# Latent down weights multiplied into the up weights on the chip, in a fused attention and feed-forward layer

## The chip, the cores and the metric

The kernel runs on one core of one Trainium2 chip. The metric is the device time of one execution in microseconds. Every number comes from timed runs of the kernel before, or from one further execution taken with the profiler.

## The reference

One transformer layer on x of 2 x 1024 tokens and 512 features, in float32: attention with 32 query heads and 8 key/value heads of 128 features, x added and normalised, then a feed-forward part of 1376 hidden features with 4-bit weights, added and normalised again. The part that matters here:

```python
q    = (x @ Wq.T)                 # 32 heads
k_r0 = x @ Wkr.T                  # 512 rope features of the keys, rotated by cos and sin
c_kv = x @ Wdk.T                  # 512 latents
k_c  = c_kv @ Wupk.T              # 512 other features of the keys
v    = c_kv @ Wupv.T              # 1024 features of the values
k    = k_c and rotated k_r0, put together
out  = softmax(causal(q @ k.T / sqrt(128))) @ v @ Wo.T
```

## The kernel before

Every product is made in three passes. A float32 matrix is split into a high part, rounded to the type that TensorE multiplies, and a low part, the rest; `three_pass` (line 262) issues high x high, high x low and low x high into one bank of PSUM. Over 512 features, four chunks of 128, that is a **group** of 12 matmuls of 128x512. Each split is a copy on ScalarE (the high part) and a subtraction on VectorE or GpSimd (the low part).

The program is written engine by engine, with semaphores between them; each engine and SyncE's queue of DMAs works through its own list strictly in order. It has three stages: projections ("a"), attention ("b") and feed-forward ("c").

**Stage a** goes over four blocks of 512 tokens (`NBLK`; `END` is the last). For block t TensorE issues 20 groups (`GROUPS_A`): four latent groups (`a_latents`, CG), four of the rope keys (RG, weights `a_wkr`), four of the other keys from the latents (NG, weights `a_wupk`; both in `a_keys`), and eight of the values (VG, weights `a_wupv`; `a_values`). Group g goes to bank `g % a_RING` of `a_bank`, five banks, and `a_group` first waits until the bank has been read (`a_bank_free`).

```python
            def a_group(t, g, pairs):

                pe.wait_ge(a_bank_free, a_count(t, g))
                three_pass(nc, a_bank[g % a_RING], pairs).then_inc(a_mm, 1)
```

The latents are split from PSUM into `a_cs` by `a_c_hi` on ScalarE and `a_c_lo` on VectorE. The rope keys are rotated on VectorE (`a_rope`, into two slots `a_kf`), rounded on ScalarE (`a_rope_hi`) and their low parts made on GpSimd (`a_rope_lo`). The other keys are split by `a_nope_hi` and `a_nope_lo`, the values by `a_v_hi` and `a_v_lo`. Keys and values go to DRAM by SyncE in pieces of 512 KB, and each block's split x too, 2 MB (`a_store_k`, `a_store_v`, `a_store_x`). SyncE's list for a block is: load the next x, store this x, then the eight stores of keys and eight of values. After block 0 it also copies x into `y_d`, DRAM to DRAM.

At the very start twelve matmuls of zeros run, then the latents of block 0 chunk by chunk as x and `Wdk` arrive (`a_first_latents`).

**The hand-over to attention.** After the last block's keys TensorE multiplies the first four query heads (`queries`), in turn with the first three value groups. The queries go to banks `bank[0]` and `bank[1]`, which are not in `a_bank`; they need the first x back from DRAM (`load_xs`) and the query weights split (`w_lo`). SyncE, when it has stored block 2's values, loads the first keys and values, the tables, two query weights (256 KB each) and x, and stores the last x. The other two query weights come after the rope keys' stores:

```python
            for n in range(8):
                a_store_k(END, n)
                if n in (1, 3):
                    load_wq(0, 2 + n // 2)
```

ScalarE's list there is `hi_wq(0, 0)`, `hi_wq(0, 1)`, `a_rope_hi(END)`, `hi_wq(0, 2)`, `hi_wq(0, 3)`, `a_nope_hi(END)`, and GpSimd's is two weight splits, four rope splits, two weight splits.

Stage b then runs 16 turns (two batches by eight key/value heads), each of scores, softmax, transposes and products with the values and `Wo`; stage c is the feed-forward part.

Of the kernel before, what the change touches and what calls it, by code (L numbers as in the profile page):

```python
# [21 lines left out]
F32 = mybir.dt.float32  # L22
# [310 lines left out]
def layer(nc, x, xT, wqT, wkrT, wdkT, wupkT, wupvT, woT, w13p, s13p, w2p, s2p, cosT, sinT, shifts,  # L333
# [5 lines left out]
    with ExitStack() as ctx:  # L339
# [6 lines left out]
        def sem(name):  # L346
# [4 lines left out]
        a_wdk = at(24 * K, "a_wdk", [P, 2, DC, 512], F32R)  # L351
# [11 lines left out]
        a_cs = at(180 * K, "a_cs", [P, 2, DC, TB], F32R)  # L363
        a_later = at(76 * K, "a_later", [P, 2, DC, 512], F32)
        a_zero = at(180 * K, "a_zero", [P, 512], F32)
# [28 lines left out]
                  tps[0][:].rearrange("p j q -> p (j q)")]  # L394
# [3 lines left out]
        a_first_in = [(sem(f"a_x0_in{k}"), sem(f"a_wdk_in{k}")) for k in range(DC)]  # L398
        a_first_hi, a_first_lo = sem("a_first_hi"), sem("a_first_lo")
        a_wkr_in = [sem(f"a_wkr_in{k}") for k in range(DC)]  # L400
        a_wkr_hi, a_wkr_lo = sem("a_wkr_hi"), [sem("a_wkr_lo0"), sem("a_wkr_lo1")]
        a_w_in = [sem(f"a_w_in{n}") for n in range(3)]
# [3 lines left out]
        a_w_hi, a_w_lo, a_wd_lo = sem("a_w_hi"), sem("a_w_lo"), sem("a_wd_lo")  # L406
# [28 lines left out]
        LATE = [(wupkT, a_later[:, 0], lambda p: a_wupk[:, p]),  # L435
                (wupvT[:, :, 0:512], a_later[:, 1], lambda p: a_wupv0[:, p]),
                (wupvT[:, :, 512:1024], a_raw[:, 0], lambda p: a_wupv1[p][:])]

        CG, RG, NG, VG, GROUPS_A = 0, 4, 8, 12, 20
        END = NBLK - 1  # L440

# [130 lines left out]
        def _(sp):  # L572
            def a_weights():
                for k in range(DC):
                    sp.dma_start(a_xraw[:, k], xT[0, :, k]).then_inc(a_first_in[k][0], 16)
                    sp.dma_start(a_raw[:, 0, k], wdkT[:, k]).then_inc(a_first_in[k][1], 16)
                for k in range(DC):
                    sp.dma_start(a_raw[:, 1, k], wkrT[:, k]).then_inc(a_wkr_in[k], 16)
                sp.dma_start(LATE[0][1], LATE[0][0]).then_inc(a_w_in[0], 16)
# [212 lines left out]
            sp.wait_ge(a_w_lo, 1)  # L792
            sp.wait_ge(a_wd_lo, 2)
# [10 lines left out]
            sp.wait_ge(a_mm, GROUPS_A * (END - 1) + RG + 4 + a_MM0)  # L804
# [41 lines left out]
        def _(pool):  # L846
# [14 lines left out]
            def a_weight_lo(n):  # L861
# [992 lines left out]
```

## Time and profile before

| | us |
|---|---|
| median of 3 timed runs | 2386.08 |
| lowest and highest | 2385.03, 2389.29 |
| the profiled execution | 2387.51 |
| its span, first to last instruction | 2385.7 |
| TensorE's matmuls busy in it | 2370.0 |
| VectorE, ScalarE, GpSimd busy | 1427.1, 1621.0, 578.6 |

The profile is of one execution. PE is TensorE's matmuls and PEld its weight loads, DVE VectorE, ACT ScalarE, POOL GpSimd, SP SyncE; SPq is the DMA queue that it issues to. A row of a timeline gives the start, the duration and the engine, then the line of the program, the operation, what it writes and reads, and how many there were; brackets at the end give the idle time before it and what ended it. An arrow points from what is read to what is written. "b_sps", "b_tps" and "b_ps" are banks of PSUM. Consecutive matmuls overlap, so the start of the next tells the pace, not the duration of one.

### The profile page before, as it was taken

How to read it: one execution, taken by the hardware profiler on the slowest of the kernel's cores; microseconds unless marked ns; L12 is line 12 of the kernel's file. 1: busy time of each engine (PE TensorE's matmuls, PEld its weight loads, DVE VectorE, ACT ScalarE, POOL GpSimd, SP SyncE). 2: the span in 40 equal slices, each digit the busy share in tenths (PEclk: the TensorE clock that was granted, in tenths of full speed). 3: DMA queues.
4: the chain of work that ended last, by engine and by line, in shares of the span. 5: the costliest groups of instructions: out<-in, count | busy, mean ns of one | idle time of the engine just before them, and what ended most of it. 6: DMA issues, size and time to landing. Idle time of an engine off the chain costs nothing.

```text
span 2385.7 us, 41133 instructions
## 1 busy us (share of the span) xinstructions
PE 2370.0 (99%) x12028; PEld 1993.1 (84%) x12028; DVE 1427.1 (60%) x3780; ACT 1621.0 (68%) x3221; POOL 578.6 (24%) x453
## 2 busy tenths in 40 slices
PE   9999999999999999999999999999999999999998
PEld 7888888888888888888888888888888888888886
DVE  5334766666767676766666676767676674242332
ACT  4224878888888888887878888888888885122211
POOL 3002323233332323232323333232323220000000
PEclk9999999999999999999999999999999999999999
DMA  7867444434353444444434445354434435311110
GB/s 273 300 216 289 131 143 138 136 132 155 131 176 110 170 138 141 132 141 149 136 129 139 148 135 174 106 171 138 148 127 145 137 129 209 120 71 36 53 35 18
DMA packets 133255, 340.24 MB, mean 143 GB/s; under 512 B 13328, under 2 KB 30736, under 8 KB 122640
## 3 DMA queue, kind: packets, MB, share of 16 engines
q1 hardware_dynamic: 133200, 339.53, 42.2%
q8 instruction: 31, 0.51, 0.1%
q14 instruction: 24, 0.20, 0.0%
HBM read 232.00 MB, written 111.67 MB: 144 GB/s over the span
## 4 chain that ended last, share of the span: by engine, by line
PE 96%; issue 1%; DVE 1%; ACT 1%; DMA 1%; SPq 0%; POOL 0%; DVEq 0%; POOLq 0%
PE b_ps L267 45%; PE b_sps L267 34%; PE b_tps L1549 10%; PE b_ps L1608 3%; PE b_tps L1608 2%; PE b_tps L267 1%; DMA b_xs<-xs_d 0%; DMA a_raw<-in_wkrT 0%; PE b_sps L1558 0%; ACT b_pt L1050 0%; ACT b_sc L1035 0%; ACT b_sc L1029 0%; DVE c_n_stats L286 0%; DVE b_sc L1252 0%; DVE a_xs L1176 0%
## 5 line engine op out<-in xcount | busy, mean ns | idle before, releaser
L1270 DVE TENSOR_TENSOR b_pt<-b_tps,b_pt 128x512 fp32r<-128x512 f32 (+3 forms) x768 | 426.8, 556 | 301.6 <-ACT b_pt L1050 297.5
L267 PE MATMUL b_sps<-b_kt,b_qs 128*128 128x512 f32 (+4 forms) x2304 | 497.1, 343 | 0.2
L1035 ACT ACTIVATE b_sc<-b_sc,b_rinv 128x896 f32<-128x896 f32 (+7 forms) x512 | 396.1, 774 | 105.4 <-DVE b_rinv L1260 99.5
L267 PEld LDWEIGHTS b_sps<-b_kt,b_qs 128*128 128x128 f32 x2304 | 403.1, 188 | 55.8 <-issue 1.4
L1050 ACT ACTIVATE b_pt<-b_tps 128x512 fp32r<-128x512 f32 (+3 forms) x768 | 366.9, 478 | 119.1 <-PE b_tps L1549 117.6
L267 PE MATMUL b_ps<-b_xs,b_wq 128*128 128x512 f32 x1536 | 441.0, 407 | 0.5 <-DMA b_xs<-xs_d 0.5
L267 PE MATMUL b_ps<-b_pt,b_vt 128*128 128x512 f32 x1584 | 436.0, 402 | 0.3 <-DVE b_ys L1281 0.3
L267 PE MATMUL b_ps<-b_wo,b_ot 128*128 128x512 f32 x1536 | 423.9, 405 | 0.1
L1029 ACT ACTIVATE b_sc<-b_sc,b_nmax 128x896 f32<-128x896 f32 (+7 forms) x512 | 395.5, 772 | 40.2 <-DVE b_nmax L1252 37.1
L1252 DVE CUSTOM_DVE_ANT_0 b_sc<-b_sps,b_mask 128x896 f32<-128x896 f32 (+7 forms) x512 | 386.7, 755 | 16.1 <-PE b_sps L267 16.0
L1549 PE MATMUL b_tps<-b_ident,b_sc 128*128 128x128 f32 x2304 | 374.3, 272 | 1.4 <-DVE b_pt L1270 1.4
L1549 PEld LDWEIGHTS b_tps<-b_ident,b_sc 128*128 128x128 f32 x2304 | 291.6, 140 | 75.9 <-issue 5.3
L267 PEld LDWEIGHTS b_ps<-b_pt,b_vt 128*128 128x128 f32 x1584 | 284.3, 188 | 49.1 <-DVE b_ys L1281 0.5
L267 PEld LDWEIGHTS b_ps<-b_xs,b_wq 128*128 128x128 f32 x1536 | 273.7, 189 | 45.9 <-DMA b_xs<-xs_d 1.6
L267 PEld LDWEIGHTS b_ps<-b_wo,b_ot 128*128 128x128 f32 x1536 | 270.8, 189 | 43.5 <-DVE b_ys L1281 0.3
L878 POOL TENSOR_TENSOR b_qs<-b_qf,b_qs 128x512 fp32r<-128x512 f32 x124 | 160.5, 1294 | 394.1 <-ACT b_qs L1009 394.1
L874 POOL TENSOR_TENSOR b_sw<-b_sw,b_sin 128x512 f32<-128x512 f32 x128 | 165.7, 1295 | 360.1 <-ACT b_sw L1002 358.7
L267 PE MATMUL b_sps<-c_xs,c_up 128*128 128x512 f32 (+3 forms) x1056 | 247.5, 390 | 0.0
L267 PEld LDWEIGHTS b_sps<-c_xs,c_up 128*128 128x128 f32 (+1 forms) x1056 | 195.2, 185 | 43.7
L1338 DVE TENSOR_TENSOR c_hb<-b_sps,c_hb 128x512 f32<-128x512 f32 (+1 forms) x44 | 30.4, 691 | 193.6 <-PE b_sps L267 187.0
L1234 DVE TENSOR_TENSOR b_qf<-b_ps,b_cos 128x512 f32<-128x512 f32 x128 | 88.5, 691 | 85.3 <-ACT b_sw L1002 43.3
L887 POOL TENSOR_TENSOR b_wo<-b_wraw,b_wo 128x512 fp32r<-128x512 f32 x64 | 82.8, 1294 | 228.6 <-ACT b_wo L1023 228.6
(133 smaller groups left out, 2271.9 us busy)
## 6 DMA issues: line engine op xcount, KB each, us to landing
b_xs<-xs_d SPq DMA_DIRECT2D x32, 2048.0 KB, 9.1
b_ys<-y_d SPq DMA_DIRECT2D x128, 256.0 KB, 2.7
y_d<-b_ys SPq DMA_DIRECT2D x128, 256.0 KB, 3.0
k_d<-a_ks SPq DMA_DIRECT2D x32, 512.0 KB, 3.9
v_d<-a_vs SPq DMA_DIRECT2D x32, 512.0 KB, 3.1
b_kt<-k_d SPq DMA_DIRECT2D x64, 256.0 KB, 4.5
b_vt<-v_d SPq DMA_DIRECT2D x16, 1024.0 KB, 4.9
b_wraw<-in_wqT SPq DMA_DIRECT2D x64, 256.0 KB, 2.7
```

What stands on the lines that cost most here:

```text
L267: ins = nc.tensor.matmul(out, *every[n], start=(n == 0), stop=(n == len(every) - 1))
L874: nc.gpsimd.tensor_tensor(sw[:], sw[:], sinq[:, blk * TB:blk * TB + TB], ALU.mult).then_inc(sin_done, 1)
L878: nc.gpsimd.tensor_tensor(qs[:, blk, h, LO], qf[:], qs[:, blk, h, HI], ALU.subtract).then_inc(q_lo, 1)
L887: nc.gpsimd.tensor_tensor(wo[:, h, LO], wraw[:, h % 2], wo[:, h, HI], ALU.subtract).then_inc(w_lo, 1)
L1029: nc.scalar.activation(sc[:, slot, 0:w], sc[:, slot, 0:w], ACT.Exp, bias=nmax[:, slot:slot + 1], scale=-1.0, accum_out=rsum[:, slot:slot + ...
L1035: nc.scalar.activation(sc[:, slot, 0:w], sc[:, slot, 0:w], ACT.Copy, scale=rinv[:, slot:slot + 1])\
L1050: nc.scalar.activation(pt[:, u % PT_UNITS, HI, 0:nj, h * P:(h + 1) * P], tps[n % 2][:, 0:nj], ACT.Copy)\
L1234: nc.vector.tensor_tensor(qf[:], banks[bk], cosq[:, blk * TB:blk * TB + TB], ALU.mult)\
L1252: nc.vector.tensor_tensor_reduce(out=like_banks(sc[:, slot, 0:w], i), in0=both_banks(sps[c % 2], i), in1=like_banks(mask[:, S - w:S], i), ...
L1270: nc.vector.tensor_tensor(pt[:, u, LO, 0:nj, h * P:(h + 1) * P], tps[n % 2][:, 0:nj], pt[:, u, HI, 0:nj, h * P:(h + 1) * P], ALU.subtract) ...
L1549: last = nc.tensor.transpose(tps[n % 2][:, j], sc[:, c % S_RING, (j0 + j) * P:(j0 + j + 1) * P], ident[:])
L1608: last = nc.tensor.matmul(c_y[t], c_hs[0:w, f % 2, a, t * P:(t + 1) * P], c_w2[f][b][0:w], start=(f == 0 and k == 0), stop=(f == FT - 1 an ...
```

## The change

The product of the down weights with each up weight is made once, at the start (`a_down_up`). TensorE transposes `Wdk` (16 transposes of 128x128), ScalarE and VectorE split it into `a_wd`, and twelve groups multiply it with the split up weights (`a_up`). Their results are split in turn into `a_wupk`, `a_wupv0` and `a_wupv1`, where the up weights themselves were. Keys and values are then multiplied from the split x (`a_x(t)`), the latent groups are gone, and a block has 16 groups instead of 20. The first products of the program are now block 0's rope keys.

The ring has eight banks, all of PSUM, the two of the queries among them. So a wait stands ahead of the queries. Because the values of block 2 now read x, the load of the queries' x (in block 2's slot) waits for those. The last block's x has a place of its own, `a_xe`. TensorE's loop over blocks 1 and 2 is written out.

```diff
-        a_cs = at(180 * K, "a_cs", [P, 2, DC, TB], F32R)
+        a_xe = at(180 * K, "a_xe", [P, 2, DC, TB], F32R)
...
         a_bank = [sps[0][:, 0:TB], sps[0][:, TB:2 * TB], sps[1][:, 0:TB], sps[1][:, TB:2 * TB],
-                  tps[0][:].rearrange("p j q -> p (j q)")]
+                  tps[0][:].rearrange("p j q -> p (j q)"), tps[1][:].rearrange("p j q -> p (j q)"),
+                  bank[0][:], bank[1][:]]
...
-        CG, RG, NG, VG, GROUPS_A = 0, 4, 8, 12, 20
+        RG, NG, VG, GROUPS_A = 0, 4, 8, 16
...
+        def a_made_bank(n, m):
+            return a_bank[m if n == 2 else 4 + m]
...
                 for k in range(DC):
                     sp.dma_start(a_xraw[:, k], xT[0, :, k]).then_inc(a_first_in[k][0], 16)
-                    sp.dma_start(a_raw[:, 0, k], wdkT[:, k]).then_inc(a_first_in[k][1], 16)
+                    sp.dma_start(a_raw[:, 1, k], wkrT[:, k]).then_inc(a_first_in[k][1], 16)
+                sp.dma_start(a_raw[:, 0], wdkT).then_inc(a_wdk_in, 16)
...
-            sp.wait_ge(a_mm, GROUPS_A * (END - 1) + RG + 4 + a_MM0)
+            sp.wait_ge(a_mm, a_count(END - 1, VG + 7) + a_MM0)
             sp.wait_ge(a_xs_out, 16 * END + a_OUT0)
             load_xs(0, 0)
...
-            def a_c_hi(t):
-                for m in range(DC):
-                    act.wait_ge(a_mm, a_count(t, CG + m) + a_MM0)
-                    nc.scalar.activation(a_cs[:, HI, m], a_bank[(CG + m) % a_RING], ACT.Copy).then_inc(a_part_hi, 1)
...
+            def a_weights_hi():
+                for k in range(DC):
+                    a_up_keys_hi(k)
+                    a_made_hi(0, k)
+                a_up_values_hi(0)
...
+            for k in range(DC):
+                a_up_keys_lo(k)
+                a_made_lo(0, k)
+            a_made_lo(1, 0)
+            a_made_lo(1, 1)
             a_rope(0)
-            a_weight_lo(2)
+            a_made_lo(1, 2)
+            a_made_lo(1, 3)
+            a_up_values_lo(1)
+            for n in (2, 3):
+                for m in range(4):
+                    a_made_lo(n, m)
...
+            def a_down_up():
+
+                pe.wait_ge(masked, 4)
+                pe.wait_ge(a_wdk_in, 16)
+                for m in range(4):
+                    for k in range(DC):
+                        last = nc.tensor.transpose(a_made_bank(0, m)[:, k * P:(k + 1) * P],
+                                                   a_raw[:, 0, m, k * P:(k + 1) * P], ident[:])
+                    last.then_inc(a_fused, 1)
+                for n in (1, 2, 3):
+                    if n == 1:
+                        pe.wait_ge(a_upk_lo, DC)
+                    else:
+                        pe.wait_ge(a_upv_lo[n - 2], 1)
+                    for m in range(4):
+                        if n == 2:
+                            pe.wait_ge(a_bank_free, a_count(0, RG + m) + a_FREE0)
+                        else:
+                            pe.wait_ge(a_fused_free, a_made(0 if n == 1 else 1, m))
+                        three_pass(nc, a_made_bank(n, m),
+                                   [(lambda p, k=k: a_wd[:, p, k, m * P:(m + 1) * P], lambda p, k=k: a_up[n - 1][:, p, k])
+                                    for k in range(DC)]).then_inc(a_fused, 1)
...
-            a_latents(END)
             a_keys(END)
-            pe.wait_ge(masked, 4)
+            pe.wait_ge(a_bank_free, a_count(END, NG + 3) + a_FREE0)
             for h in range(GQ):
                 if h >= 2:
                     pe.wait_ge(q_cos, h - 1)
                 queries(0, 0, h, h % 2, 0, products("q0", h))
```

How the order of TensorE's instructions moves, first at the start of the program. Before (`a_wdk`, `a_wkr` are weights, `a_zero` the zeros, brackets name the semaphores waited for):

```order
L1502 MATMUL b_tps<-a_zero 128x512 x11
L267 MATMUL b_sps<-a_xs,a_wdk 128x512 [waits a_first_lo]
L267 MATMUL b_sps<-a_xs,a_wdk 128x512 x11
...
L267 MATMUL b_tps<-a_xs,a_wkr 128x512 [waits a_bank_free,a_wkr_lo1,a_wkr_lo0]
```

and with the change:

```order
L267 MATMUL b_sps<-a_xs,a_wkr 128x512 [waits a_first_lo]
L267 MATMUL b_sps<-a_xs,a_wkr 128x512 x11
L1547 MATMUL b_tps<-b_ident,a_raw 128x128 [waits a_wdk_in,b_masked]
L1547 MATMUL b_tps<-b_ident,a_raw 128x128 x7
L1547 MATMUL b_ps<-b_ident,a_raw 128x128 x8
L267 MATMUL b_tps<-a_upk,a_wd 128x512 [waits a_fused_free,a_upk_lo]
L267 MATMUL b_tps<-a_upk,a_wd 128x512 x11
```

The latents of block 0 are gone; the rope keys stand in their place, and transposes and weight products follow.

Second, TensorE at the hand-over, from the last groups of the last block's keys (`a_wupk`) to the first query (`b_wq`). Before:

```order
L267 MATMUL b_sps<-a_cs,a_wupk 128x512 [waits a_bank_free]
L267 MATMUL b_sps<-a_cs,a_wupk 128x512 x11
L267 MATMUL b_ps<-b_xs,b_wq 128x512 [waits b_w_lo,b_xs_in,b_masked]
L267 MATMUL b_ps<-b_xs,b_wq 128x512 x11
L267 MATMUL b_sps<-a_wupv_60,a_cs 128x512 [waits a_bank_free]
```

and with the change:

```order
L267 MATMUL b_ps<-a_xe,a_wupk 128x512 [waits a_bank_free]
L267 MATMUL b_ps<-a_xe,a_wupk 128x512 x11
L267 MATMUL b_ps<-b_xs,b_wq 128x512 [waits b_w_lo,b_xs_in,a_bank_free]
L267 MATMUL b_ps<-b_xs,b_wq 128x512 x11
L267 MATMUL b_sps<-a_wupv_60,a_xe 128x512 [waits a_bank_free]
```

The last keys now write the banks of the queries, and the first query waits for `a_bank_free`.

Third, ScalarE's list with the change at the same place, from the last copy of block 2's values (`a_vs`) on:

```order
L992 ACTIVATE a_vs<-b_ps 128x4x128 [waits a_v_out1,a_mm]
L1039 ACTIVATE b_wq<-b_wraw 128x512 [waits b_w_in0]
L1039 ACTIVATE b_wq<-b_wraw 128x512 [waits b_w_in1]
L981 ACTIVATE a_ks<-a_kf 128x512 [waits a_rope_done,a_k_out0]
...
L981 ACTIVATE a_ks<-a_kf 128x512 [waits a_rope_done,a_k_out3]
L1039 ACTIVATE b_wq<-b_wraw 128x512 [waits b_w_in0]
L1039 ACTIVATE b_wq<-b_wraw 128x512 [waits b_w_in1]
L987 ACTIVATE a_ks<-b_tps 128x512 [waits a_mm,a_k_out0]
...
L987 ACTIVATE a_ks<-b_ps 128x512 [waits a_mm,a_k_out3]
```

Here only the four copies of latents ahead of the first `b_wq` are gone; the rest stands in the order of before.

## Rows read from the trace of the kernel before

**Rows 1.** The page, part 1: busy time, share, instructions

```profile
PE 2370.0 (99%) x12028; PEld 1993.1 (84%) x12028; DVE 1427.1 (60%) x3780; ACT 1621.0 (68%) x3221; POOL 578.6 (24%) x453
```

**Rows 2.** The page, part 4: the chain that ended last, by engine

```profile
PE 96%; issue 1%; DVE 1%; ACT 1%; DMA 1%; SPq 0%; POOL 0%; DVEq 0%; POOLq 0%
```

**Rows 3.** TensorE's waits, whole span: total us, times, longest

```profile
PE b_tps L1502 <- POOL a_zero L847: 1.5, 1, 1.5
...
PE b_sps L267 <- DVE a_ks L1206: 1.0, 1, 1.0
```

**Rows 4.** TensorE's timeline, block 1: latents, first rope keys

```profile
62.84 11.04 PE L267 MATMUL b_sps<-a_xs,a_wdk 128*128 x48
73.72 2.88 PE L267 MATMUL b_tps<-a_xs,a_wkr 128*128 x12
```

**Rows 5.** TensorE's timeline, attention: three and four transposes

```profile
256.11 0.49 PE L1549 MATMUL b_tps<-b_ident,b_sc 128*128 128x128 f32 x3
...
259.20 0.60 PE L1549 MATMUL b_tps<-b_ident,b_sc 128*128 128x128 f32 x4
```

**Rows 6.** TensorE's timeline, start: zeros, first rope keys

```profile
1.53 4.94 PE L1502 MATMUL b_tps<-a_zero 128*128 128x512 f32 x12 [1.53 <-POOL a_zero L847]
...
18.08 2.88 PE L267 MATMUL b_tps<-a_xs,a_wkr 128*128 128x512 f32 x12
```

**Rows 7.** Timelines of VectorE, ScalarE and GpSimd, 16 to 33 us

```profile
16.87 2.74 DVE L1181 TENSOR_TENSOR a_cs<-b_sps,a_cs 128x512 fp32r<-128x512 f32 x4 [1.40 <-ACT a_cs L959]
...
19.14 1.92 ACT L938 ACTIVATE a_wupk<-a_later 128x2048 fp32r<-128x2048 f32 x1 [0.25 <-DMA a_later<-in_wupkT]
...
28.32 4.63 POOL L864 TENSOR_TENSOR a_wupv<-a_later,a_wupv 128x2048 fp32r<-128x2048 f32 x1 [11.60 <-ACT a_wupv L938]
```

**Rows 8.** The end: TensorE's timeline; engines by stretch (PEclk: granted clock)

```profile
2372.69 2.94 PE L1608 MATMUL b_ps<-c_w,c_hs 128*128 128x512 f32 x12
...
2378.00:2379.00 1.00, 0.00 (x0) 0.00 (x0) 0.34 (x2) 0.20 (x1) 0.00 (x0) 0.50 0.00 0
```

**Rows 9.** TensorE's timeline: last block's latents, first query

```profile
171.64 11.04 PE L267 MATMUL b_sps<-a_xs,a_wdk 128*128 128x512 f32 x48
...
204.28 2.88 PE L267 MATMUL b_ps<-b_xs,b_wq 128*128 128x512 f32 x12
```

**Rows 10.** VectorE's timeline: last two splits of the last keys

```profile
207.95 1.28 DVE L1206 TENSOR_TENSOR a_ks<-b_sps,a_ks 128x512 fp32r<-128x512 f32 x2
```

**Rows 11.** SyncE's DMA queue, hand-over: keys, then query weights

```profile
174.12 2.06 SPq L634 DMA_DIRECT2D b_kt<-k_d  x4
...
177.63 0.91 SPq L617 DMA_DIRECT2D b_wraw<-in_wqT  x2
...
195.06 0.62 SPq L617 DMA_DIRECT2D b_wraw<-in_wqT  x1
...
199.62 0.63 SPq L617 DMA_DIRECT2D b_wraw<-in_wqT  x1
```

**Rows 12.** ScalarE's timeline, hand-over: first and last query weights

```profile
187.27 1.30 ACT L1015 ACTIVATE b_wq<-b_wraw 128x512 fp32r<-128x512 f32 x2 [3.96 <-DMA b_wraw<-in_wqT]
...
205.60 0.63 ACT L1015 ACTIVATE b_wq<-b_wraw 128x512 fp32r<-128x512 f32 x1 [2.60 <-DMA b_wraw<-in_wqT]
```

**Rows 13.** GpSimd's timeline, hand-over: weight splits, rope splits

```profile
187.98 2.55 POOL L882 TENSOR_TENSOR b_wq<-b_wraw,b_wq 128x512 fp32r<-128x512 f32 x2 [43.34 <-ACT b_wq L1015]
191.89 2.55 POOL L869 TENSOR_TENSOR a_ks<-a_kf,a_ks 128x512 fp32r<-128x512 f32 x2 [1.36 <-ACT a_ks L969]
196.47 2.54 POOL L869 TENSOR_TENSOR a_ks<-a_kf,a_ks 128x512 fp32r<-128x512 f32 x2 [2.04 <-ACT a_ks L969]
```

**Rows 14.** Engines by stretch; the last three columns: PEclk, DMA share, GB/s

```profile
174.00:202.00 28.00, 28.00 (x125) 23.18 (x124) 11.37 (x16) 6.12 (x10) 7.64 (x6) 1.00 1.01 369
202.00:206.00 4.00, 4.00 (x19) 3.32 (x18) 0.00 (x0) 1.03 (x2) 1.28 (x1) 1.00 0.49 173
```

**Rows 15.** The page, part 6: DMA issues, KB each, us to landing

```profile
b_wraw<-in_wqT SPq DMA_DIRECT2D x64, 256.0 KB, 2.7
```

**Rows 16.** ScalarE's timeline, block 1: first other-key copy

```profile
93.78 0.60 ACT L975 ACTIVATE a_ks<-b_sps 128x512 fp32r<-128x512 f32 x1 [3.78 <-DMA k_d<-a_ks]
```

More of the change, by code:

```diff
@@ L993, in a_block_of @@
                     a_v_hi(t, n, a_bank[(VG + n) % a_RING])
-                    for _ in range(3 if n < 4 else 2):
+                    for _ in range(4 if n < 4 else 4):
                         act.sem_inc(placed, 1)
+                a_rope_hi(t + 1)
             def swap_q(it, blk, h, bk):
@@ L1140, in _ @@
             a_first_split()
-            a_block_of(0, True)
-            for t in range(1, END):
-                a_block_of(t, False)
-            a_c_hi(END)
+            a_weights_hi()
+            for t in range(END - 1):
+                a_block_of(t)
+            a_x_split(END)
+            a_nope_hi(END - 1)
+            for n in range(8):
+                a_v_hi(END - 1, n, a_bank[(VG + n) % a_RING])
             hi_wq(0, 0)
@@ L1503, in a_first_latents @@
                                      start=True, stop=True)
-                pairs = [a_project(lambda p: a_wdk[:, p], m, a_xs[:, 0]) for m in range(4)]
+                pairs = [a_project(lambda p: a_wkr[:, p], m, a_xs[:, 0]) for m in range(4)]
                 for k in range(DC):
@@ L1519, in a_keys, with a_latent_keys @@
+            def a_latent_keys(t):
                 for m in range(4):
[L1520 to L1525 removed]
+                    if type(t) is int and t == 0:
+                        pe.wait_ge(a_fused_free, a_made(3, m))
+                    a_group(t, NG + m, a_project(lambda p: a_wupk[:, p], m, a_x(t)))
@@ L1699, in late_values @@
             def late_values(a, bk, lo, hi):
-                ins = three_pass(nc, banks[bk], a_values(a), lo, hi)
+                ins = three_pass(nc, banks[bk], a_values(END, a), lo, hi)
                 if hi == products("va", a):
@@ L1749, in a_all_values @@
                 for n in range(8):
-                    if n == 0:
-                        pe.wait_ge(a_w_lo, 1)
-                    if n == 1:
-                        pe.wait_ge(a_wd_lo, 2)
-                    a_group(t, VG + n, a_values(n))
-            a_first_latents()
-            a_keys(0)
+                    a_group(t, VG + n, a_values(t, n))
+            a_first_keys()
+            a_down_up()
+            a_latent_keys(0)
             a_all_values(0)
-            with pe.Fori(1, END) as t:
-                a_latents(t)
+            for t in range(1, END):
                 a_keys(t)
                 a_all_values(t)
-            a_latents(END)
             a_keys(END)
-            pe.wait_ge(masked, 4)
+            pe.wait_ge(a_bank_free, a_count(END, NG + 3) + a_FREE0)
             for h in range(GQ):
@@ L1770, in _ @@
                 if h < V_LATE:
-                    a_group(END, VG + h, a_values(h))
+                    a_group(END, VG + h, a_values(END, h))
             turns(pe, turn_of)
```

159 lines of the change are left out of this document (78 added, 81 removed).

## The prediction

> **What bounds the kernel now.** I read the page's list of engines first [rows 1]: TensorE's matmuls are busy for 2370.0 of 2385.7 us. The chain of work that ended last is TensorE for 96% [rows 2]. The list of what TensorE waited for [rows 3] is short and sorted: its first entry, the wait for the start, is 1.5 us, and all others are smaller. So whatever leaves TensorE's queue shortens the run, and whatever makes it wait lengthens it, one for one. The timeline of the projection stage [rows 4] shows the pace: the 48 matmuls of block 1's latents take 11.04 us and the 12 of its first keys 2.88, so 36 more cost 8.16: 0.227 us a matmul, 2.72 a group of twelve, 54.4 a block of 20 groups. The profiled execution took 2387.51 us, 1.4 above the median of the three runs, 2386.08; I sum against the former and move the result by that.
>
> **Work removed and added.** Gone are the latents: four groups in each of four blocks, 16 x 2.72 = 43.5 us. Added once are twelve groups in a_down_up, 12 x 2.72 = 32.6 us, and 16 transposes of 128x128. Four transposes in a row take 0.60 us and three take 0.49 [rows 5], so one costs 0.11 and sixteen cost 1.8. Net: -43.5 + 32.6 + 1.8 = **-9.1 us**. The Trainium skill (TensorE: Matmul & The Clock Gate, Back-to-back issue gap) gives a warm gap of N/2.4 + 2.5 ns, 56 ns at 128 columns. By that estimate the transposes would cost 0.9 us and the net be -10.0; the trace's 0.11 us a transpose disagrees, and I keep it.
>
> The ScalarE and VectorE copies of the latents go too, and 16 pairs of copies for the made weights come. Both engines have room, busy 68% and 60% of the span [rows 1]. The copies count only where TensorE waits for them, which is at two places. The old wait of 1.0 us inside block 0, for a_ks [rows 3], goes: eight banks instead of five stand between a group and the one that reuses its bank, and the values wait for rope, done long before.
>
> **The start: a new chain of small steps.** Before, the products with the first x end at 18.08 and the keys follow at once [rows 6]. Now the first keys end at the same 18.1 (the same bytes arrive, wkr for wdk), the transposes end at 19.9, and the next group needs four pieces of a_upk split on both engines plus a_made_lo(0, 0). ScalarE and VectorE alternate piece and transposed bank: the first transposed bank can be copied at 18.8, then come three pairs. VectorE does four such pieces in 2.74 us [rows 7], 0.65 a step with the last one's tail taken off, and ScalarE keeps up with that. VectorE starts at 19.4 and needs six steps to the last a_upk piece: 19.4 + 6 x 0.65 = 23.3. TensorE waits 23.3 - 19.9 = **3.4 us**. Bounds: 2.0 if the pieces are all split before the transposes are ready, 4.5 if a piece of a_upk lands late (the old wupk was copied at 19.14 [rows 7], after as many bytes as stand ahead of its last piece now). The later weights are covered: each is ready 2.72 us after the last, GpSimd's 4.63 us split of the values [rows 7] starts near 25 and TensorE needs it at 34, and rope frees bank 0 at about 31, needed at 34.
>
> **The clock.** In the first 4.94 us twelve matmuls ran [rows 6]; later twelve take 2.88 [rows 6]. That is the level of 1.2 GHz at first, and the way back to 2.4 cost 2.06 us. At the end the last matmul ends at 2375.63 and the granted clock reads 0.50, 1.2 GHz, in the stretch from 2378 on [rows 8]: it fell within 2.4 us of TensorE's stop. A wait of 3.4 us is longer, so I take one loss of 2.06 us at the start, with 0 as the other bound. The Trainium skill (same page, the part on the HAM clock gate) says that an idle TensorE returns to 1.2 GHz and a busy one regains 2.4; the trace's last rows agree, and this speaks against the change at each new wait.
>
> **The hand-over to attention, the largest term.** The ring of banks now takes in the two banks that the queries use. So TensorE must wait, after the last block's latent keys, until VectorE has read bank NG+3 (a_nope_lo(END), fourth). Before, the first query started at once at 204.28 [rows 9], while the last of those splits ended only at 207.95 + 1.28 = 209.23 [rows 10], and TensorE needed none of it yet. They are late because ScalarE works in order. Count from E, the start of TensorE's last block (171.64 before [rows 9]); the number before is the trace's, the number now is mine:
> - SyncE starts the attention loads at E + 2.5 (174.12) and the queries' first two weights at E + 6.0; x halves and x store follow. They queue behind 2 MB of keys and values and 1 MB of tables [rows 11]; ScalarE gets them at 187.27 = E + 15.6 [rows 12]. The same loads are issued at the same distance now, so E + 15.6 again.
> - ScalarE's rope copies stand behind those, at E + 16.9, and GpSimd's rope splits behind its two weight splits (187.98 + 2.55 = E + 18.9 [rows 13]). Before, the key products were as late; now they have long been ready.
> - The weight of head 2 is asked for 3.2 us after the rope splits start (191.89 to 195.06): E + 22.1. The third split starts at E + 21.7 because a_kf has two slots, and head 3's weight is asked for 3.2 us later (196.47 to 199.62): E + 24.8, against E + 28.0 before.
> - It landed at 205.60 = E + 34.0 [rows 12]. The DMA engines are full from 174 to 202, and half busy until 206 [rows 14]. The bytes are the same, so I take E + 33.0. Bounds: E + 27.5 (2.7 us, the median of this load on an ordinary turn [rows 15]) and E + 34.0.
> - From there to the end of the fourth a_nope_lo: 209.23 - 205.60 = 3.6 us [rows 10, 12], so E + 36.6.
>
> TensorE is ready at E + 8 x 2.72 = E + 21.8. It waits **14.9 us** (9.4 to 15.8) and then starts cold, 2.06 us more. Nothing queued behind can fill it: queries and late values stand after that wait on its queue. The load of the queries' x now also waits for block 2's values, but those end at E, before SyncE comes to that load, so it costs nothing.
>
> **Sum:** -9.1 + 3.4 - 1.0 + 2.1 + 14.9 + 2.1 = +12.4 us, so 2399.9 for the profiled execution and 2398.5 for the median.
>
> **Rivals.**
> 1. *The queue is short and the change wins.* If the first weights land in 2.7 us, rope follows the key products, head 3's weight is asked for at E + 17.9 and lands at E + 20.6, and only the last copy pair stands behind TensorE, about 1.5 us. Then -9.1 + 3.4 - 1.0 + 1.5 = -5.2, 2380.9; with a clock loss at the start -3.1. It decides where the hand-over wait and all clock losses are together under 6.7 us. For it: 43.5 us a block instead of 54.4 lets no load be issued later. Against: 8.5 us of the chain is DMA backlog that this change does not touch [rows 14]. Chance 0.12.
> 2. *Only the last load is quick:* wait 9.4 instead of 14.9, +6.9, 2393.0; without clock losses +2.8. Chance 0.08.
> 3. *The clock holds* through the short pause or both: +10.3 or +8.3, 2396.4 or 2394.4. Chance 0.12.
> 4. *Block 1 stalls too.* The copy of x into y_d is issued after block 0, and block 1's key stores queue behind it: the first latent-key copy waited for such a store until 93.78 [rows 16], so its split ended near 95.1, 32.3 us after the block's start at 62.84. Now the fifth value group needs that bank 12 x 2.72 = 32.6 us after the start. A margin of 0.3 us; if it slips by 3 us: +15.1, 2401.2. Chance 0.10.
>
> **How the numbers follow.** The main case has 0.58. 0.2% is 4.8 us, about what a measurement of this kernel can tell from no change. Slower by more: main, 3, 4 and half of 2, 0.84. Within: 0.08 (half of 2, and of 1 the share with a cold start). Faster: 0.08. The range goes from all low bounds with the clock held (-9.1 + 2.0 - 1.0 + 9.4 = +1.3, 2387.5) to all high ones with rival 4 (-9.1 + 4.5 - 1.0 + 15.8 + 4.1 + 2.7 = +17.0, 2403). Rival 1 and a little above the top are left out.
>
> **What the profile should show.** 144 matmuls from a_upk and a_upv between about 23 and 58, 16 transposes ending near 20, no a_cs. TensorE starts block 3 (a_xe) near 178, stops near 200 for about 15 us with VectorE's a_ks as releaser, and its first matmuls after it take twice as long. I am wrong if that pause is under 7 us, if ScalarE's last two b_wq copies come before the latent keys' end, or if the value groups show waits.

## The result, and the profile after

| | before | after |
|---|---|---|
| median, us | 2386.08 (3 runs) | 2398.32 (4 runs) |
| lowest and highest | 2385.03, 2389.29 | 2397.54, 2400.57 |
| the profiled execution | 2387.51 | 2400.57 |
| its span | 2385.7 | 2398.8 |

The changed kernel takes 1.0048 times as long, 95% interval 1.0036 to 1.006: some 12 us slower, and clear of the spread of the runs. The forecast was 2398.5. One more run of the kernel before, of 8483.18 us, is not among its three.

The page of the changed kernel, part 1 (busy time by engine) and the start of part 4 (the chain that ended last):

```profile
PE 2365.4 (99%) x11996; PEld 1989.4 (83%) x11996; DVE 1422.9 (59%) x3781; ACT 1618.1 (67%) x3220; POOL 573.9 (24%) x451
...
PE 87%; ACT 1%; DVE 1%; issue 1%; DMA 1%; POOL 0%; SPq 0%; DVEq 0%; ACTq 0%; POOLq 0%
```

TensorE has less to do than before, 2365.4 instead of 2370.0 us [rows 1], and the run is longer: what is longer is idle time, 33.4 us of the span instead of 15.7. The share of the chain says nothing of it. It has gone from 96% [rows 2] to 87%, but 18 us are under 1% of the span, and x8 below, with hardly a wait, has 88%. TensorE's waits in the changed kernel (total us, times, longest):

```profile
PE b_ps L267 <- DVE a_ks L1242: 14.1, 1, 14.1
PE b_tps L267 <- DVE a_upk L1207: 3.1, 1, 3.1
PE b_sps L267 <- DVE a_wkr L1476: 2.0, 1, 2.0
```

Against [rows 3] the first two are new, the first at the hand-over and the second at the start, and the 1.0 us for a_ks inside block 0 is gone. The third was 0.58 us before. TensorE's timeline at both places:

```profile
8.10 12.76 PE L267 MATMUL b_sps<-a_xs,a_wkr 128*128 128x512 f32 x48 [2.04 <-DVE a_wkr L1476]
20.70 1.03 PE L1547 MATMUL b_tps<-b_ident,a_raw 128*128 128x128 f32 x8
21.57 1.04 PE L1547 MATMUL b_ps<-b_ident,a_raw 128*128 128x128 f32 x8
25.71 7.16 PE L267 MATMUL b_tps<-a_upk,a_wd 128*128 128x512 f32 x24 [3.10 <-DVE a_upk L1207]
32.70 5.60 PE L267 MATMUL b_ps<-a_upk,a_wd 128*128 128x512 f32 x24
...
179.58 11.04 PE L267 MATMUL b_sps<-a_xe,a_wkr 128*128 128x512 f32 x48
190.46 5.60 PE L267 MATMUL b_tps<-a_xe,a_wupk 128*128 128x512 f32 x24
195.90 5.60 PE L267 MATMUL b_ps<-a_xe,a_wupk 128*128 128x512 f32 x24
215.63 4.98 PE L267 MATMUL b_ps<-b_xs,b_wq 128*128 128x512 f32 x12 [14.13 <-DVE a_ks L1242]
220.45 2.90 PE L267 MATMUL b_sps<-a_wupv,a_xe 128*128 128x512 f32 x12
```

The last block starts at E = 179.58, and TensorE is through with its keys 21.9 us later. Then it does nothing until VectorE's last split of a_ks. The granted clock beside it (the row is a stretch, the busy time and count of each engine, then the clock, the share of DMA and GB/s):

```profile
206.00:208.00 2.00, 0.00 (x0) 0.00 (x0) 0.00 (x0) 0.00 (x0) 0.00 (x0) 0.55 1.05 402
208.00:214.00 6.00, 0.00 (x0) 0.00 (x0) 0.91 (x2) 2.68 (x6) 2.53 (x2) 0.50 0.59 227
...
218.00:220.00 2.00, 2.00 (x7) 1.57 (x6) 0.00 (x0) 0.00 (x0) 0.00 (x0) 0.53 1.01 383
220.00:222.00 2.00, 2.00 (x10) 1.65 (x9) 0.00 (x0) 1.19 (x2) 0.00 (x0) 1.00 0.30 104
```

The clock is at 2.4 GHz in the first 4.5 us of the pause (1.00 from 202 to 206), then at 1.2 GHz for the rest of it and for nearly all of the first query, so that query takes 220.45 - 215.63 = 4.82 us instead of 2.72. What the last split waited for stands in the timelines of VectorE, ScalarE and the queue:

```profile
214.30 1.28 DVE L1242 TENSOR_TENSOR a_ks<-b_ps,a_ks 128x512 fp32r<-128x512 f32 x2
```

```profile
195.25 1.30 ACT L1039 ACTIVATE b_wq<-b_wraw 128x512 fp32r<-128x512 f32 x2 [14.87 <-DMA b_wraw<-in_wqT]
196.45 1.13 ACT L981 ACTIVATE a_ks<-a_kf 128x512 fp32r<-128x512 f32 x2
201.64 1.23 ACT L981 ACTIVATE a_ks<-a_kf 128x512 fp32r<-128x512 f32 x2 [4.05 <-DVE a_kf L1237]
208.77 0.63 ACT L1039 ACTIVATE b_wq<-b_wraw 128x512 fp32r<-128x512 f32 x1 [5.89 <-DMA b_wraw<-in_wqT]
211.95 0.63 ACT L1039 ACTIVATE b_wq<-b_wraw 128x512 fp32r<-128x512 f32 x1 [2.55 <-DMA b_wraw<-in_wqT]
212.48 1.06 ACT L987 ACTIVATE a_ks<-b_tps 128x512 fp32r<-128x512 f32 x2
```

```profile
201.62 0.62 SPq L638 DMA_DIRECT2D b_wraw<-in_wqT  x1
...
205.43 0.65 SPq L638 DMA_DIRECT2D b_wraw<-in_wqT  x1
```

The products that the key copies (L987) read were done at 201.5, and the copies stood on ScalarE's list behind head 3's weight: asked for at E + 25.9, there at E + 32.4 ("there" and "landed" are the start of ScalarE's copy, which the load's end released). These rows answer to [rows 11, 12].

### The profile page after: what moved, and what is told of

Its sections match the earlier page's. It is cut to its first block, busy times and chain, and to the rows that moved or that the text cites. A ratio compares the mean times of both kernels' runs of the same rounds, so it can differ in the third digit from the quotient of the medians.

```text
span 2398.8 us, 41007 instructions
## 1 busy us (share of the span) xinstructions
PE 2365.4 (99%) x11996; PEld 1989.4 (83%) x11996; DVE 1422.9 (59%) x3781; ACT 1618.1 (67%) x3220; POOL 573.9 (24%) x451
## 4 chain that ended last, share of the span: by engine, by line
PE 87%; ACT 1%; DVE 1%; issue 1%; DMA 1%; POOL 0%; SPq 0%; DVEq 0%; ACTq 0%; POOLq 0%
PE b_ps L267 44%; PE b_sps L267 28%; PE b_tps L1603 10%; PE b_ps L1662 3%; PE b_tps L1662 2%; DMA b_kt<-k_d 0%; ACT b_sc L1053 0%; ACT b_pt L1074 0%; PE b_sps L1612 0%; ACT b_sc L1059 0%; DMA b_wraw<-in_wqT 0%; DVE b_pt L1300 0%; DVE b_sc L1282 0%; SPq L655 0%; DVE c_n_stats L286 0%
## 5 line engine op out<-in xcount | busy, mean ns | idle before, releaser
L267 PE MATMUL b_ps<-b_xs,b_wq 128*128 128x512 f32 x1536 | 442.7, 408 | 14.1 <-DVE a_ks L1242 14.1
L1264 DVE TENSOR_TENSOR b_qf<-b_ps,b_cos 128x512 f32<-128x512 f32 x128 | 88.5, 691 | 92.5 <-ACT b_sw L1026 50.5
```

What stands on the lines that cost most here:

```text
L267: ins = nc.tensor.matmul(out, *every[n], start=(n == 0), stop=(n == len(every) - 1))
L1264: nc.vector.tensor_tensor(qf[:], banks[bk], cosq[:, blk * TB:blk * TB + TB], ALU.mult)\
```

## Experiments

E is the start of the last block's 48 rope-key matmuls in each run; diffs are against the changed kernel, whose median was 2398.32. A ratio is to the kernel before, with its 95% interval. The kernel before had medians of 2387.33 beside the first four runs, 2386.11 beside the next four, 2386.81 beside x9 and x10 and 2386.52 beside x11 and x12.

**The start (x1_pieces_first).**

```diff
                 for k in range(DC):
                     a_up_keys_hi(k)
+                for k in range(DC):
                     a_made_hi(0, k)
```

and the same on VectorE, with `a_up_keys_lo` and `a_made_lo`.

> The changed kernel with one order changed at the start: ScalarE and VectorE split all four pieces of a_upk first and the four transposed banks of Wdk after them, instead of in turn. Theory (TensorE's 3.1 us wait after the transposes is the in-turn order: it needs the fourth piece of a_upk, six VectorE steps after the first transposed bank, and this pause also costs half-clock time): now only one copy and one subtraction stand between the transposes and the next group, so the wait is 1.2 to 1.6 us, the clock stays up, and the median is 1.6 + 1.5 to 2 us lower than the 2398.3 of the change: 2394.5 to 2395.5. Rival (the pieces arrive late, so that the order does not matter): wait 3 us as before and 2398.3.

2394.68 us, ratio 1.0033 (1.0022 to 1.0045), 3.6 less than the change. TensorE's timeline there:

```profile
20.23 5.72 PE L267 MATMUL b_tps<-a_upk,a_wd 128*128 128x512 f32 x24 [0.20 <-DVE a_wd L1218]
```

The wait is 0.2 us instead of 3.1 (1.2 to 1.6 expected), and the 24 matmuls behind it run at the full clock. The alternation of pieces and transposed banks was the cause, and the cost is a matter of order alone: wait and half clock were 4.4 us in the profile and 3.6 by the medians.

**Does the pause cost a clock, too? (x2_filler, x7_filler_64).** Matmuls whose products nobody reads, and which are overwritten, fill most of the pause; 56 in one run and 64 in the other.

```diff
+            pe.wait_ge(a_bank_free, a_count(END, RG) + a_FREE0)
+            for n in range(56):
+                nc.tensor.matmul(a_bank[0], a_wkr[:, HI, n % DC, 0:P], a_xe[:, HI, n % DC], start=True, stop=True)
             pe.wait_ge(a_bank_free, a_count(END, NG + 3) + a_FREE0)
```

> The changed kernel with 56 matmuls of 128x512 put on TensorE's queue in front of the wait at the hand-over. They write bank 0, which the next group overwrites, so nobody reads them; 56 x 0.227 = 12.7 us of the 14.1 us pause. Theory (the pause itself is set by other engines, and the half-clock stretch after it costs another 2.1 us): the first query starts at the same distance from the last block's start, 36 us, at full clock, its twelve matmuls take 2.9 us instead of 5.0, and the median is 2396.2. Rival (the slow first matmuls after the pause have another cause, for example the arriving x and stores): they stay at 5 us and the median at 2398.3. Second rival (the extra matmuls delay something): above 2398.3.

> The same as the filler with 56 matmuls, but 64 (14.5 us), because there a pause of 2.8 us was left and the twelve matmuls of the first query still took 4.6 us. The products are overwritten and read by nobody. Theory (the pause alone brings the half-clock stretch, and one of 2.8 us is already enough): the pause left is under 1.5 us, the first query's twelve matmuls take 2.9 us, and the median is 1.7 to 2.1 lower than with 56 fillers. Rival (the slow twelve have another cause): 4.6 us again.

TensorE's timeline with 56 fillers, then with 64:

```profile
198.76 12.85 PE L1816 MATMUL b_sps<-a_xe,a_wkr 128*128 128x512 f32 x56
214.45 4.61 PE L267 MATMUL b_ps<-b_xs,b_wq 128*128 128x512 f32 x12 [2.84 <-DVE a_ks L1242]
218.90 2.92 PE L267 MATMUL b_sps<-a_wupv,a_xe 128*128 128x512 f32 x12
```

```profile
198.44 14.67 PE L1816 MATMUL b_sps<-a_xe,a_wkr 128*128 128x512 f32 x64
214.18 3.01 PE L267 MATMUL b_ps<-b_xs,b_wq 128*128 128x512 f32 x12 [1.07 <-DVE a_ks L1242]
217.03 2.88 PE L267 MATMUL b_sps<-a_wupv,a_xe 128*128 128x512 f32 x12
```

With 2.84 us of pause left the first query takes 4.45 us to the start of the next group, with 1.07 us left 2.85. So the clock's price is real and is 1.6 us here and 2.1 in the change. The times don't show it: 2399.53 us (1.0037 to 1.0071) and 2396.84 us (1.0029 to 1.0063) overlap. I had expected 2396.2 with 56 fillers. Instead the last split came at E + 37.5 instead of E + 36.0 in both runs, and by the first scores that had cost more than the clock gave back with 56 fillers (60.98 us from E, 59.93 in the change) and most of it with 64 (59.39). Head 3's weight landed 1.4 us later than in the change, and it did so too in x3 below (E + 33.9), which has no fillers but also keeps TensorE at work there. Why is not shown.

**Is it the bank? (x3_query_banks_apart).** In the last block the ring has six banks, so the queries' two are free, and the new wait goes.

```diff
+        def a_place(t, g):
+            return a_bank[g % (6 if type(t) is int and t == END else a_RING)]
...
-            pe.wait_ge(a_bank_free, a_count(END, NG + 3) + a_FREE0)
             for h in range(GQ):
```

> The changed kernel, but in the last block only the groups go round six banks, so that the queries' two banks are free, and the wait ahead of the first query is gone. Theory (the ring of eight banks at the last block is what holds TensorE 14.1 us, but the same late ScalarE list stands behind it): the first two queries and value groups run at once; then the third query, which reuses the first one's bank, waits for the first query's cosine product, which stands on ScalarE's and VectorE's lists behind the last block's key copies, at 37 us after the block's start against 32.6: a new wait of 4 to 5 us and one half-clock stretch of 2 us. Median 2398.3 - 14.1 + 5 = 2389 to 2390. Rival A (nothing takes its place): 2398.3 - 14.1 - 2.1 = 2382. Rival B (TensorE is held at the same point by something else, w_lo or x): 2398.

2392.68 us, ratio 1.0023 (1.0013 to 1.0033): 5.6 less than the change, and 3 more than I expected. TensorE's timeline:

```profile
199.21 2.88 PE L267 MATMUL b_ps<-b_xs,b_wq 128*128 128x512 f32 x12
...
204.65 2.88 PE L267 MATMUL b_ps<-b_xs,b_wq 128*128 128x512 f32 x12
...
216.11 4.41 PE L267 MATMUL b_ps<-b_xs,b_wq 128*128 128x512 f32 x12 [5.85 <-DVE b_qf L1267]
```

The first two queries go at once, and the third waits 5.85 us, because the first one's bank is read by VectorE (b_qf) only after the same late splits of a_ks. So the bank is where the lateness meets TensorE first, and without it TensorE meets the same lateness four groups later, half clock included. From E to the first scores this kernel takes 8.9 us less than the change, and from there to the end 3.5 more (2162.8 against 2159.3). Two waits of 0.95 and 1.20 us close behind the first scores, which the change does not have, are 2.2 of them; the rest stays open.

**Where does the lateness come from? (x4 to x6).** Three single moves: ScalarE's key copies ahead of the weights of heads 2 and 3; the first two query weights ahead of the reload; the last x stored after the rope keys.

```diff
-            hi_wq(0, 2)
-            hi_wq(0, 3)
             a_nope_hi(END)
+            hi_wq(0, 2)
+            hi_wq(0, 3)
```

```diff
+            load_wq(0, 0)
+            load_wq(0, 1)
             for slot in range(4):
                 sp.wait_ge(a_k_out[slot], 16 * 2 * 2)
             load_k(0)
...
-            load_wq(0, 0)
-            load_wq(0, 1)
```

```diff
-            a_store_x(END)
             for n in range(8):
                 a_store_k(END, n)
                 if n in (1, 3):
                     load_wq(0, 2 + n // 2)
+                if n == 3:
+                    a_store_x(END)
```

> The changed kernel, but ScalarE makes the last block's four key copies before the copies of the third and fourth query weight instead of after them. Theory (ScalarE's in-order list and the weights' late landing hold the copies): now they wait only until the rope keys' stores have landed, about 30 to 31 us after the last block's start instead of 33; the wait at the hand-over is 10.5 to 12.5 us instead of 14.1, the median 2394.5 to 2397. Rival (the key copies are bound by those stores anyway): wait 14 us, 2398.3. Rival (the weights alone hold them): the wait falls to under 5 us, 2389.

> The changed kernel, but SyncE asks for the first two query weights before it asks for the first keys, values and tables, instead of after them; the bytes are the same. Two readings of the chain at the hand-over are told apart. Bytes (the DMA engines are full from 3 to 28 us after the last block's start, and the fourth query weight lands when the queue has run dry, whenever it was asked for): the rope splits come 7 to 9 us earlier, the fourth weight is asked for near 17 instead of 26 us, but lands only 1 to 3 us earlier than 32.4, the wait of 14.1 us becomes 11 to 13, the median 2395 to 2397.5. Steps (the chain of in-order copies sets it): the weight lands 7 to 9 us earlier, the wait becomes 5 to 7 us, the median 2389 to 2391.

> The changed kernel, but SyncE stores the last block's x (2 MB) after the fourth query weight has been asked for, instead of before the rope keys' stores. Bytes: 2 of the 10 MB ahead of that weight are gone, some 5 us at 0.4 MB a us, but it is still asked for at 26 us, so it lands at 28.5 to 30 us instead of 32.4 and the wait is 10 to 12 us instead of 14.1; median 2394 to 2396. Steps alone: the load of the weight takes the same 6 us after it is asked for, wait 14.1, median 2398.3.

x4: 2395.15 us (1.0023 to 1.0048), wait 11.4. x5: 2400.32 us (1.0043 to 1.0077), wait 14.8. x6: 2398.45 us (1.003 to 1.0064), wait 13.1. Only the first is worth anything, and it as expected. Its ScalarE shows what the copies wait for when the weights are not ahead of them:

```profile
203.63 0.60 ACT L987 ACTIVATE a_ks<-b_tps 128x512 fp32r<-128x512 f32 x1 [4.15 <-DMA k_d<-a_ks]
...
208.21 0.60 ACT L987 ACTIVATE a_ks<-b_ps 128x512 fp32r<-128x512 f32 x1 [0.66 <-DMA k_d<-a_ks]
```

The rope keys' stores have to leave the slots of a_ks first, and they let the last copy start at E + 31.9. So in the change the late weights cost only 2.8 us more (14.1 against 11.4) than this second tie costs by itself. The prediction does not name it.

x5 and x6 missed: neither reading of x5 allowed 14.8 (11 to 13, or 5 to 7), and x6's 13.1 lies between its two (10 to 12, or 14.1). Why x5 gave nothing stands in its queue and in ScalarE's timeline:

```profile
192.96 4.16 SPq L617 DMA_DIRECT2D k_d<-a_ks  x2
197.17 4.29 SPq L638 DMA_DIRECT2D b_wraw<-in_wqT  x1
```

```profile
183.28 0.63 ACT L1039 ACTIVATE b_wq<-b_wraw 128x512 fp32r<-128x512 f32 x1 [5.29 <-DMA b_wraw<-in_wqT]
...
210.26 0.63 ACT L1039 ACTIVATE b_wq<-b_wraw 128x512 fp32r<-128x512 f32 x1 [2.62 <-DMA b_wraw<-in_wqT]
```

The first weight is there at E + 6.1 instead of E + 15.7, rope follows it, and head 3's weight is asked for at E + 20.0, 6 us earlier. The issue alone takes 4.29 us, and the weight lands at E + 33.1, no earlier than in the change. In x6 the first weights are there only at E + 17.2, and head 3's, with 2 MB fewer ahead of it, is asked for at E + 27.4 and lands 4.0 us later.

**Both at once, and a place for the keys (x9_both_loads, x10_both_and_place).** x9 has the edits of x5 and x6. In x10 the last block's other keys also have a buffer of their own, a_ke, so that their copies wait for no store of the rope keys:

```diff
+        a_ke = at(108 * K, "a_ke", [P, 4, 2, TB], F32R)
...
-                    act.wait_ge(a_k_out[n], 16 * (2 * t + 1))
+                    if t != END:
+                        act.wait_ge(a_k_out[n], 16 * (2 * t + 1))
```

> The edits of the two runs before this one are made together: the first two query weights are asked for ahead of the reload of keys and values, and the last x is stored after the fourth rope key. Theory 'steps and bytes take turns': with the store alone the late chain of steps set the wait (13.1 us), with the weights alone the full queue did (14.8); together the rope splits go as early as with the weights alone, the last query weight is asked for near E + 20 and lands some 4 us later, and the wait falls to 5 to 9 us; the time is 2389 to 2394 us. Theory 'each change has a price of its own': 0 and 1 us add up, the wait stays at 12 to 14 us and the time at 2397 to 2398 us.

> As the run beside it, and the last block's other-key copies have a place of their own, so that they wait for no store of the rope keys. If those stores hold the copies back once the weights come early, the wait falls by 2 us or more against the run beside it, to 2 to 6 us, and the time is 2386 to 2391 us. If only the last query weights stand ahead of the copies, the place gives nothing: the wait and the time are those of the run beside it, within 1 us.

x9: 2396.93 us (1.0026 to 1.0054), wait 11.1, where I expected 5 to 9; x10: 2396.26 us (1.0024 to 1.0052), wait 11.2, so the place alone gives nothing. The queue and ScalarE's timeline of x9:

```profile
194.42 2.67 SPq L638 DMA_DIRECT2D b_wraw<-in_wqT  x1
```

```profile
190.56 1.23 ACT L982 ACTIVATE a_ks<-a_kf 128x512 fp32r<-128x512 f32 x2 [3.71 <-DVE a_kf L1238]
202.76 0.63 ACT L1040 ACTIVATE b_wq<-b_wraw 128x512 fp32r<-128x512 f32 x1 [10.97 <-DMA b_wraw<-in_wqT]
206.08 0.63 ACT L1040 ACTIVATE b_wq<-b_wraw 128x512 fp32r<-128x512 f32 x1 [2.69 <-DMA b_wraw<-in_wqT]
```

Both theories were wrong about this one. Head 3's weight is asked for at E + 17.7, ahead of the x store, and still takes 11.7 us. ScalarE then stands idle for 10.97 us with the key copies behind it. In these five kernels, all with the weights ahead of the copies, one sum gives the wait: TensorE's wait is the landing of head 3's weight, plus the 3.6 us of the prediction's last step, minus the 21.8 us at which TensorE is ready.

| | asked for | landed | + 3.6 - 21.8 | wait measured |
|---|---|---|---|---|
| the change | E + 25.9 | E + 32.4 | 14.2 | 14.1 |
| x5 | E + 20.0 | E + 33.1 | 14.9 | 14.8 |
| x6 | E + 27.4 | E + 31.4 | 13.2 | 13.1 |
| x9 | E + 17.7 | E + 29.4 | 11.2 | 11.1 |
| x10 | E + 17.6 | E + 29.5 | 11.3 | 11.2 |

Asking 10 us earlier with the same bytes ahead (x9 and x10 against x6) brings it 2 us earlier, and asking 6 us earlier (x5 against the change) not at all. So asking earlier hardly hurries these loads; TensorE's wait has to be taken off them.

**Off the queue (x11_weights_and_keys_first, x12_rework_x_store_early, x8_handover_rework).** x11 has the edits of x4 and x5. x12 has those of x1, x4 and x5 and a_ke; x8 is x12 with x6's late store too, and ran before it.

> The changed kernel with the pieces first at the start, and the hand-over reworked: the first two query weights asked for before keys and values, the last x stored after the fourth query weight was asked for, the last block's other-key copies put in a place of their own (the free slot of x), so that they wait for no store, and made before the copies of the third and fourth query weight. Theory (the whole loss is the in-order ScalarE list, the slots of a_ks and the queue): the wait at the hand-over is the last copy and subtraction, 1.3 to 2 us, with no slow matmuls after it, and the start saves its 3.6: 2398.3 - 3.6 - 12.5 - 2.1 = 2380, 6 us under the kernel before. Rival (another wait takes its place: the load of the queries' x, w_lo of the first heads, or the copies of the first turn as in the run with the query banks apart): 2383 to 2388.

> Two lists are reordered and nothing else: the first two query weights are asked for ahead of the reload, and ScalarE copies the last block's other keys before the weights of heads 2 and 3. Theory 'late weights in a full queue': with the early rope chain what holds TensorE is only that the key copies stand behind weights that land 10 us after they are asked for; then the wait falls to under 4 us, no half clock follows it, and the time is 2383 to 2387 us. Rival 'the slots': the copies then wait for the rope keys' stores out of the same a_ks slots, which go through the same full queue and leave it some 8 to 12 us after they are asked for (near E + 16 and E + 20): then the wait stays at 7 to 11 us and the time at 2391 to 2395 us.

> The rework of the earlier run, but with the last x stored where the change stores it. With the early rope chain, the key copies ahead of the late weights and a place of their own for them, nothing that TensorE waits for at the hand-over goes through the full queue any more: 'late weights in a full queue' and 'the slots' both expect a wait of 1 to 2.5 us and 2380 to 2383 us, as with the late store. If the 2 MB still decide, the wait is over 4 us and the time above 2385 us.

x11: 2397.15 us (1.0025 to 1.005), wait 12.8: my theory fell. The rival's mechanism is what the rows show, but its sizes (7 to 11 us, 2391 to 2395) were too small as well. ScalarE's timeline of x11:

```profile
207.19 0.60 ACT L987 ACTIVATE a_ks<-b_tps 128x512 fp32r<-128x512 f32 x1 [13.77 <-DMA k_d<-a_ks]
...
211.79 0.60 ACT L987 ACTIVATE a_ks<-b_ps 128x512 fp32r<-128x512 f32 x1 [0.64 <-DMA k_d<-a_ks]
```

Now the copies wait for the stores out of the a_ks slots, which go through the same queue: 13.77 us for the first one, and the last starts at E + 33.3. x8 takes both ties away, as expected (2380): 2381.17 us, ratio 0.998 (0.9971 to 0.999), faster than the kernel before by 4.9 us and than the change by 17. TensorE's waits there, and its timeline:

```profile
PE b_ps L267 <- DVE a_ke L1252: 1.4, 1, 1.4
...
PE b_tps L267 <- DVE a_wd L1227: 0.2, 1, 0.2
```

```profile
195.78 3.02 PE L267 MATMUL b_ps<-b_xs,b_wq 128*128 128x512 f32 x12 [1.41 <-DVE a_ke L1252]
198.64 2.88 PE L267 MATMUL b_sps<-a_wupv,a_xe 128*128 128x512 f32 x12
```

The wait is 1.4 us, only the last pair of copies, and the clock holds over it: 2.86 us from the first query to the next group. x12 isolates the late store: 2387.07 us, ratio 1.0 (0.999 to 1.0009), where I expected 2380 to 2383. Its first wait is 1.4 us as well, but its timelines of TensorE, the queue and ScalarE show another:

```profile
209.95 5.49 PE L267 MATMUL b_ps<-b_xs,b_wq 128*128 128x512 f32 x12 [3.05 <-DVE b_qf L1273]
215.24 3.26 PE L267 MATMUL b_sps<-a_wupv,a_xe 128*128 128x512 f32 x12
```

```profile
193.65 4.30 SPq L643 DMA_DIRECT2D b_wraw<-in_wqT  x1
197.99 4.30 SPq L622 DMA_DIRECT2D k_d<-a_ke  x4
```

```profile
203.93 0.63 ACT L1046 ACTIVATE b_wq<-b_wraw 128x512 fp32r<-128x512 f32 x1 [8.99 <-DMA b_wraw<-in_wqT]
207.15 0.63 ACT L1046 ACTIVATE b_wq<-b_wraw 128x512 fp32r<-128x512 f32 x1 [2.58 <-DMA b_wraw<-in_wqT]
```

The late weights now hold up ScalarE's copies of the first query's rope, which are next on its list, and through them the bank of the third query: 3.05 us, then 5.29 + 3.09 us for two groups instead of 5.44, together 6.0, which is the 5.9 between the two medians. In x8 head 3's weight is there 28.8 us after E, in x12 34.8 (with E = 172.4 in both), and in x8 nothing waits.

## Why the prediction was right

The mechanism was right: the two new waits came where they were forecast, for the reasons given, and the second is the larger by far. That the time fits to 0.2 us is in part luck, as the terms show. From the profiled execution before to the one after the span grew by 13.1 us; the medians differ by 12.2.

| term | forecast | measured |
|---|---|---|
| groups and transposes | -9.1 | -9.0 |
| wait in front of a_down_up | +3.4 | +3.1 |
| half clock behind it | +2.1 | +1.55 |
| old wait for a_ks | -1.0 | -1.0 |
| wait at the hand-over | +14.9 | +14.1 |
| half clock behind it | +2.1 | +2.1 |
| first keys later | none | +2.6 |
| sum | +12.4 | +13.4 |

The sum is what TensorE has lost when the first scores start (226.04 before, 239.51 after); from there to the end both take the same, 2159.7 and 2159.3 us.

- **Work.** 144 made matmuls stand between 25.71 and 59.90, no group reads a_cs, and the pace is 0.227 us. The sixteen transposes take 25.71 - 3.10 - 20.70 = 1.91 us (1.8 forecast). The Trainium skill (TensorE: Matmul & The Clock Gate, Back-to-back issue gap) gives 56 ns at 128 columns for an isolated matmul and about 81 ns in a stream with weight loads; the eight from 20.70 to 21.57 took 0.109 us each, so the trace disagrees with both, as [rows 5] did.
- **The start.** The mechanism was as put, and x1 shows it. VectorE's steps took 0.60 us each and not 0.65, hence 3.1 us and not 3.4. The half clock behind it was sized a little high: 24 matmuls took 32.70 - 25.71 = 6.99 us instead of 5.44. The 2.06 of the forecast came from the pace of the first twelve matmuls alone; the granted clock reads 1.00 over them (2 to 6 us, before), so no row of the clock stands behind that size.
- **The hand-over.** First weights forecast at E + 15.6 and seen at E + 15.7; head 2's asked for at E + 22.1 and E + 22.0; head 3's at E + 24.8 and E + 25.9, landed E + 33.0 and E + 32.4; the last split ended at E + 36.6 and E + 36.0. The landing was the estimated step: it was chosen near the landing of before, and came 0.6 us earlier. That it came so near is partly luck. In other kernels with the x store ahead of that load it landed between E + 32.7 and E + 34.8, and x5 and x9 show that it hardly depends on when it is asked for. The forecast also knew only the weight as a cause; the stores out of a_ks would have held the copies nearly as long (x4).
- **Not forecast: +2.6 us at the first keys.** In this execution the first rope keys waited 2.04 us, not 0.58 as the first products did before, and then ran partly at half clock, 12.60 us to the next group instead of 11.03 before (to the 18.08 of [rows 6]). The granted clock there is 0.59 from 10 to 12 us. In the profiles of the twelve later kernels, which start alike up to there, the keys waited 0 to 1.33 us and kept the clock, and the transposes began between 17.5 and 18.8 and not at 20.70. So it is chance of one execution, which was 2.4 us above the median of the other three. I had no term for it. Without it the rows sum to +10.8, and the profiled execution before was 1.4 us above its median: that makes the 12.2 between the medians. So the forecast's waits and clock losses were 1.6 us too high, and the median it added them to was 1.4 us lower than the execution that its rows come from; the two nearly cancel.
- **Rivals.** Rival 1 (the queue is short, 2380.9) did not happen. Its wait of 1.5 us for the last copy pair is what x8 reaches (1.4 measured), but with head 3's weight still 11.4 us on its way, by taking the wait off the queue. Rival 2 fell: the last load took 6.5 us, not 2.7. Rival 3 fell in both pauses. Rival 4 did not happen: no value group of block 1 waits. The first other-key copy came at 120.65 in a block that started near 92.5, so after 28.1 us and not after the 30.9 of [rows 16], and the margin was some 3 us instead of 0.3.

After the result my sizes for the hand-over failed in x5, x6, x9, x11 and x12. In x5, x6 and x9 I expected the last weight earlier than it came, for being asked for earlier or for fewer bytes ahead of it. In x11 I expected the wait to go with the weights, but the stores of the rope keys were nearly as late. In x12 I had not counted the late weights in front of the copies of the first query.

What stays open: between x8 and the kernel before the sum would give -9.1 - 1.0 + 0.2 + 1.4 = -8.5 us; the first scores start 8.4 us earlier, the profiled executions differ by 7.8 in span, the medians by 4.9. The last two differ because the profiled execution before lies 1.4 us above its median and that of x8 1.5 below; which of the executions is the typical one, the traces can't say.

## What to carry to other kernels

When a change shares a buffer that was private before, ask who reads it last and what stands ahead of that reader on its engine's list, not how long the read takes: the last copy of 0.6 us started 12 us after its product here, behind the copy of a weight that nobody needed yet, and with that out of the way still 10 us after it, because its slot was still being stored (x4). On an in-order engine put what frees a resource ahead of what waits for a full DMA queue; in the backed-up queue here, asking 10 us earlier for a load moved its landing by 2. And remove all ties to the queue at once when trying this: each alone gave 3.2 us at most (x4), all together 13.5 (x8 against x1).

## What the hardware showed that I had not expected

- **Issuing can block.** The issue of one 256 KB load took 4.29 us on the queue's row in x5, against 0.62 in [rows 11]. In x12 it took 4.30, and the stores of a_ke behind it, the first of which had its data at 188.6, went out only at 197.99. Full DMA engines are not enough for this: in the change they were as full (share 1.02) when the same issue took 0.62 us at 201.62. The slow ones (2.2 to 4.3 us) are in the kernels that ask for the first weights early; what decides is not shown.
- **Landing goes with the backlog.** Head 3's weight took 4.0 us (asked for at E + 27.4, x6), 6.5 (E + 25.9, the change), 11.7 (E + 17.7, x9) and 13.1 (E + 20.0, x5). In the seven kernels where it can be read with the 2 MB of x ahead of it, it landed between E + 32.4 and E + 34.8; in the four with them behind it, between E + 28.8 and E + 31.4.
- **The clock.** TensorE lost the full clock after idle times of 2.04 and 3.10 us (start of the changed kernel's profile), 2.84 (x2) and 3.05 (x12), and kept it over 1.07 (x7), 1.33 (x6, start) and 1.41 (x8). The groups behind a loss cost 1.5 to 3.0 us more than at the full clock; the highest are x11's start and x12's third query. The Trainium skill (the same page, the part on the HAM clock gate) says that an idle TensorE falls to 1.2 GHz and a busy one regains 2.4 GHz, and the rows agree.
